# A decoder layer on one core: the last chunk of its sparse FFN selected and summed by tile of 128 rows, and the last batch's window projection issued one head pair per unit

## What is computed

```
h = silu(x @ w_gate) * (x @ w_up)            # 256 x 1024 per batch
g = h.reshape(B, S, I // 4, 4)
_, idx = top_k(abs(g), 2)                    # the two largest of each four
h_sparse = g, with all but those two at zero
out = x + h_sparse @ w_down                  # 1024 -> 256
```

## Time and profile before

| | |
|---|---|
| three runs | 408.34, 408.43 (median), 408.79 us |
| the profiled execution | 408.79 us |
| its span, first to last instruction | 406.9 us |
| mean granted TensorE clock | 0.999 of full |
| busy: PE, PEld, DVE, ACT, POOL | 95%, 78%, 71%, 53%, 42% of the span |
| share of the chain that ended last | PE 54%, DVE 21%, issue 8%, POOL 8%, ACT 7%, DMA 1%, SPq 1% |

### The profile page before, as it was taken

How to read it: one execution, slowest core, us unless ns; L and a number is a source line. 1 busy time by engine, 2 the same in 40 slices (tenths; PEclk the granted TensorE clock), 3 DMA queues, 4 the chain that set the end, 5 groups by cost and what they waited for, 6 DMA issues and landing times.

```text
span 406.9 us, 8265 instructions
## 1 busy us (share of the span) xinstructions
PE 387.9 (95%) x3060; PEld 317.9 (78%) x3060; DVE 288.2 (71%) x616; ACT 214.1 (53%) x546; POOL 169.5 (42%) x168
## 2 busy tenths in 40 slices
PE   8997899799999999999999999999999999998996
PEld 8776778667799877877789877877778779865895
DVE  4986922788859974678959976488867973675373
ACT  1474834397443752287544663186734836187330
POOL 5562698577611430267620440166831420066000
PEclk9999999999999999999999999999999999999999
DMA  7995430213000400343000410243001300200000
GB/s 202 362 346 148 121 117 26 82 50 92 10 15 17 139 2 3 102 118 85 2 15 0 128 31 0 79 119 83 2 2 52 105 0 3 80 0 2 27 0 27
DMA packets 33175, 28.39 MB, mean 70 GB/s; under 512 B 18672, under 2 KB 28016, under 8 KB 32880
## 3 DMA queue, kind: packets, MB, share of 16 engines
q1 hardware_dynamic: 33136, 27.87, 22.3%
HBM read 18.95 MB, written 4.98 MB: 59 GB/s over the span
## 4 chain that ended last, share of the span: by engine, by line
PE 54%; DVE 21%; issue 8%; POOL 8%; ACT 7%; DMA 1%; SPq 1%; POOLq 0%; DVEq 0%; ACTq 0%
PE ps L658 12%; PE ps L739 8%; PE ps L598 5%; DVE rope L966 4%; ACT prob L1394 4%; POOL prob L1255 4%; PE ps L524 3%; DVE mx L996 3%; PE ps L755 3%; PE ps L619 3%; PE ps L533 3%; DVE total L1010 2%; DVE rope L963 2%; PE ps L644 2%; PE ps L697 2%
## 5 line engine op out<-in xcount | busy, mean ns | idle before, releaser
L1255 POOL TENSOR_TENSOR prob<-prob,inv 128x512 f32<-128x512 f32 x80 | 82.7, 1041 | 81.4 <-DVE inv L1016 81.4
L1394 ACT ACTIVATE prob<-ps,mx 128x128 f32<-128x128 f32 (+1 forms) x128 | 52.6, 429 | 16.4 <-DVE mx L994 13.2
L658 PE MATMUL ps<-wo_sb,qs 128*128 128x256 f32 x256 | 59.6, 379 | 0.0
L1248 POOL TENSOR_TENSOR qs<-rope 128x512 f32<-128x512 f32 x32 | 40.8, 1275 | 41.6 <-DVE rope L966 37.7
L598 PE MATMUL ps<-ident_sb,prob 128*128 128x128 f32 x320 | 49.8, 278 | 4.9 <-POOL prob L1255 4.3
L658 PEld LDWEIGHTS ps<-wo_sb,qs 128*128 128x128 f32 x256 | 46.9, 190 | 6.7 <-issue 1.4
L1404 ACT ACTIVATE pT<-ps 128x512 f32<-128x512 f32 x76 | 45.6, 600 | 10.7 <-PE ps L598 10.1
L966 DVE TENSOR_TENSOR rope<-ps,trig_sb 64x512 f32<-64x512 f32 x70 | 48.2, 688 | 0.9
L598 PEld LDWEIGHTS ps<-ident_sb,prob 128*128 128x128 f32 x320 | 36.5, 140 | 13.9 <-POOL prob L1255 9.9
L1231 POOL TENSOR_TENSOR rstd<-vareps,power 128x1 f32<-128x1 f32 x24 | 13.2, 553 | 67.7 <-DVE vareps L945 67.4
L994 DVE TENSOR_REDUCE mx<-ps 128x2 f32<-128x512 f32 (+1 forms) x48 | 32.7, 689 | 9.0 <-PE ps L578 8.1
(11 more groups left out here) (164 smaller groups left out, 798.7 us busy)
## 6 DMA issues: line engine op xcount, KB each, us to landing
k<-kx SPq DMA_DIRECT2D x32, 128.0 KB, 2.9
q<-qx SPq DMA_DIRECT2D x28, 128.0 KB, 2.5
vb<-v_sb SPq DMA_DIRECT2D x42, 64.0 KB, 2.1
work<-in_wgu SPq DMA_DIRECT2D x4, 512.0 KB, 7.8
wo_sb<-in_wo SPq DMA_DIRECT2D x1, 2048.0 KB, 13.4
vb<-v_sb SPq DMA_DIRECT2D x36, 32.0 KB, 2.8
wq_raw<-in_wqk SPq DMA_DIRECT2D x2, 512.0 KB, 7.9
wd_sb<-in_wd SPq DMA_DIRECT2D x1, 1024.0 KB, 7.3
```

The source lines that it names most:

```text
L658: mm = pe.matmul(half_banks(use, b)[:, 0, :], window_o[t][:, pair, r, :], wo_sb[:, pair, r, :], start=(pair == 0 and r == 0), stop=(pair = ...
L1248: pool.tensor_tensor(to, cos, sin, ALU.add).then_inc(s_sums, 1)
L1255: pool.tensor_tensor(p, p, inv[:, i % ND, 0:g].unsqueeze(2).broadcast_to([P, g, 512 // g]), ALU.mult).then_inc(s_norm, 1)
L1394: ins = act.activation(prob[:, i % ND, h * k:(h + 1) * k], ps[:, BANK_S + i % 2, h * k:(h + 1) * k], ACT.Exp, bias=mx[:, i % ND, h:h + 1], ...
```

## The change

It has two parts. In the last batch's window phase, `window_out` of the first tile is called once per round i = 8 to 11, as in the other batches. And the last chunk of the last batch is handled by tile t of 128 rows from the second half of its products on: DVE multiplies lanes 2 and 3 tile by tile, ACT takes their magnitudes tile by tile, DVE compares each tile in four instructions, TensorE adds the ranks of each tile in two banks of its own, DVE keeps each tile, TensorE projects each tile into a bank of its own, DVE adds each and SP writes each. The idle matmuls of the last selection become one, between the two tiles' ranks; the first chunk's projection goes tile by tile too.

```diff
--- before.py
+++ after.py
@@ -75,7 +75,7 @@
 OUT0_AT = 10
 
 IDLE_UNITS = {13: 1, 14: 1}
-IDLE = {"scores": 2, "values": 1, "transposes": 1, "gates": 1, "ranks": 3, "last": 1}
+IDLE = {"scores": 2, "values": 1, "transposes": 1, "gates": 1, "ranks": 1}
 
 HELD_AT = 2
 
@@ -111,6 +111,9 @@
 FFN_BANKS = [(o, i % NF) for i, o in enumerate(FFN_ORDER[:n])]
 FFN_BANKS += [(("gate10", HELD), 0), (("gate11", HELD), 1), (("up11", HELD), 2)]
 FFN_BANKS += [(o, i % NF) for i, o in enumerate(FFN_ORDER[n:])]
+
+LAST_SUMS = ("down", "down_second")
+FFN_BANKS += [((LAST_SUMS[1], B - 1), dict(FFN_BANKS)["gate11", B - 1])]
 FFN_PLACE = {o: (NM + k, sum(l == k for _, l in FFN_BANKS[:i])) for i, (o, k) in enumerate(FFN_BANKS)}
 
 
@@ -313,7 +316,8 @@
             return ps[:, BANKS_M[k] if k < NM else BANK_PT + k - NM, :]
 
 
-        rank_banks = [ps[:, BANKS_M[k], :].rearrange("p (t n) -> p t n", t=2) for k in (0, 2)]
+        rank_banks = [[ps[:, k, 0:2 * P].rearrange("p (t n) -> p t n", t=2) for k in banks]
+                      for banks in ((BANKS_M[0], BANKS_M[2]), (BANK_S, BANK_S + 1))]
 
         def half_banks(name, b):
             return bank(name, b).rearrange("p (t n) -> p t n", t=2)
@@ -474,9 +478,10 @@
                     latents(b + 2)
                 if b + 1 < B:
                     cross_keys(b + 2)
-            wait_drained(sp, "down", B - 1)
-            sp.dma_start(out[B - 1].rearrange("(t p) d -> p t d", p=P), rows[B - 1]).then_inc(s_out, 16)
-            sp.wait_ge(s_out, 16 * B)
+            for t, use in enumerate(LAST_SUMS):
+                wait_drained(sp, use, B - 1)
+                sp.dma_start(out[B - 1][t * P:(t + 1) * P, :], rows[B - 1][:, t]).then_inc(s_out, 16)
+            sp.wait_ge(s_out, 16 * (B + 1))
 
         @block.tensor
         def _(pe):
@@ -758,14 +763,27 @@
                 if 3 in lanes and (c or b < HELD):
                     mm.then_inc(filled(*use), 1)
 
-            def ranks():
+            def down_tile(c, t):
+
+                b, use, tile = B - 1, LAST_SUMS[t], slice(t * P, (t + 1) * P)
+                if c == 0:
+                    claim(use, b)
+                for j in range(4):
+                    pe.wait_ge(s_kept, 4 * (FC * b + c) + (4 * t if c else 0) + j + 1)
+                    mm = pe.matmul(half_banks(use, b)[:, t, :], hidden[b][c][:, j, tile], wd_sb[:, c * 4 + j, :],
+                                   start=(c == 0 and j == 0), stop=(c == 1 and j == 3), skip_group_check=True)
+                if c:
+                    mm.then_inc(filled(use, b), 1)
+
+            def ranks(t):
 
                 pe.wait_ge(s_minus, 1)
-                pe.wait_ge(s_beats, FC * B)
-                b01, b23, b02, b13, b03, b12 = (beats[:, k, :] for k in range(6))
-                first, second = rank_banks
-                pe.matmul(first, ident_bf[:], beats[:, 2:4, :], start=True, stop=False, skip_group_check=True)
-                pe.matmul(first, ident_bf[:], beats[:, 4:6, :], start=False, stop=False, skip_group_check=True)
+                pe.wait_ge(s_beats, FC * B + t)
+                b01, b23, b02, b13, b03, b12 = (beats[:, k, t * P:(t + 1) * P] for k in range(6))
+                first, second = rank_banks[t]
+                pe.matmul(first, ident_bf[:], beats[:, 2:4, t * P:(t + 1) * P], start=True, stop=False, skip_group_check=True)
+                pe.matmul(first, ident_bf[:], beats[:, 4:6, t * P:(t + 1) * P], start=False, stop=False,
+                          skip_group_check=True)
                 pe.matmul(first[:, 0, :], ident_bf[:], b01, start=False, stop=True, skip_group_check=True)
                 pe.matmul(first[:, 1, :], minus_bf[:], b01, start=False, stop=True, skip_group_check=True)\
                   .then_inc(s_ranks, 1)
@@ -791,12 +809,8 @@
                         unit_transpose(b, i - LAG_T)
                     if i == NQB + LAG_V - 1 and more:
                         transpose_norm("ln1", b, 3 * b + 2)
-                    if i >= NQB and more:
+                    if i >= NQB:
                         window_out(b, 0, pair=i - NQB)
-                    elif NQB <= i < NQB + 3:
-                        if i == NQB:
-                            window_out(b, 0, pair=0)
-                        window_out(b, 0, pair=i - NQB + 1)
                     if i >= LAG_V:
                         unit_values(b, i - LAG_V)
                 n = 3 * b + (3 if more else 2)
@@ -892,11 +906,13 @@
                     unit_scores(b + 1, 2)
                     down(b, 0, (2, 3))
                 else:
-                    down(b, 0)
+                    for t in range(TT):
+                        down_tile(0, t)
+                    ranks(0)
                     idle(IDLE["ranks"], BANK_S)
-                    ranks()
-                    idle(IDLE["last"], BANK_S)
-                    down(b, 1)
+                    ranks(1)
+                    for t in range(TT):
+                        down_tile(1, t)
 
             pe.wait_ge(s_warm, 1)
             for _ in range(WARM):
@@ -1023,27 +1039,38 @@
                 dve.tensor_tensor(h, h, half_banks(f"up{c}{j}", b), ALU.mult)\
                    .then_inc(drained(f"up{c}{j}", b), 1)
 
-            def compare(b, c):
+            def last_values(t):
+
+                b, tile = B - 1, slice(t * P, (t + 1) * P)
+                wait_filled(dve, "up11", b)
+                wait_drained(dve, "gate11", b)
+                h = hidden[b][1][:, 2:4, tile]
+                dve.tensor_tensor(h, h, half_banks("up11", b)[:, :, tile], ALU.mult).then_inc(drained("up11", b), 1)
+
+            def compare(b, c, t=None):
 
                 n = FC * b + c + 1
                 mag, to = mags[b][c], held_beats if (b, c) == (HELD, 1) else beats
-                dve.wait_ge(s_mag, 2 * n)
+                if t is not None:
+                    mag, to = (x[:, :, t * P:(t + 1) * P] for x in (mag, to))
+                dve.wait_ge(s_mag, 2 * n + (t or 0))
                 dve.tensor_tensor(to[:, 0:2, :], mag[:, 0::2, :], mag[:, 1::2, :], ALU.is_ge)
                 dve.tensor_tensor(to[:, 2:4, :], mag[:, 0:2, :], mag[:, 2:4, :], ALU.is_ge)
                 dve.tensor_tensor(to[:, 4, :], mag[:, 0, :], mag[:, 3, :], ALU.is_ge)
                 dve.tensor_tensor(to[:, 5, :], mag[:, 1, :], mag[:, 2, :], ALU.is_ge).then_inc(s_beats, 1)
 
-            def keep(src, b, c, lanes=range(4)):
+            def keep(src, b, c, lanes=range(4), rows_of=slice(0, S)):
                 for j in lanes:
                     op, least = ((ALU.is_ge, 2.0), (ALU.is_ge, 1.0), (ALU.is_ge, 0.0), (ALU.is_le, 1.0))[j]
-                    h = hidden[b][c][:, j, :]
+                    h = hidden[b][c][:, j, rows_of]
                     dve.scalar_tensor_tensor(h, src[j], least, h, op, ALU.mult).then_inc(s_kept, 1)
 
-            def keep_last():
+            def keep_last(t):
 
                 for k in range(2):
-                    dve.wait_ge(s_ranks, k + 1)
-                    keep([rank_banks[j // 2][:, j % 2, :] for j in range(4)], B - 1, 1, (2 * k, 2 * k + 1))
+                    dve.wait_ge(s_ranks, 2 * t + k + 1)
+                    keep([rank_banks[t][j // 2][:, j % 2, :] for j in range(4)], B - 1, 1, (2 * k, 2 * k + 1),
+                         slice(t * P, (t + 1) * P))
 
             def pair_sums(b, c, beats, part):
                 n = FC * b + c + 1
@@ -1191,14 +1218,22 @@
                     chunk_values(b, 0, j)
                 if b != HELD:
                     sparsify(b, 0)
-                    for j in range(2):
-                        chunk_values(b, 1, j)
+                    chunk_values(b, 1, 0)
+                    if more:
+                        chunk_values(b, 1, 1)
                 if more:
                     first_units(b + 1, b)
                 else:
-                    compare(b, 1)
-                    keep_last()
-                    add_out("down", b, b)
+                    for t in range(TT):
+                        last_values(t)
+                    for t in range(TT):
+                        compare(b, 1, t)
+                    for t in range(TT):
+                        keep_last(t)
+                    for t, use in enumerate(LAST_SUMS):
+                        wait_filled(dve, use, b)
+                        dve.tensor_tensor(rows[b][:, t], half_banks(use, b)[:, t, :], rows[b][:, t], ALU.add)\
+                           .then_inc(drained(use, b), 1)
 
             dve.memset(warm, 0.0).then_inc(s_warm, 1)
             dve.memset(kd[:, :, :, 0:WIN], 0.0)
@@ -1449,6 +1484,13 @@
                     act.wait_ge(s_beats, FC * b + c)
                 act.activation(mags[b][c][:, 2 * j:2 * j + 2, :], hidden[b][c][:, 2 * j:2 * j + 2, :], ACT.Abs)\
                    .then_inc(s_mag, 1)
+
+            def last_magnitudes(t):
+
+                k, n = ring_use("up11", B - 1)
+                act.wait_ge(s_drained[k], n + 1 + t)
+                tile = slice(t * P, (t + 1) * P)
```

(7 more changed lines are left out.)

## The result

The changed kernel took 406.08 us in the median (405.84 to 407.13, 6 runs), the one before 408.61 beside it (408.34 to 409.93, 6 runs): ratio 0.9935, 95% interval 0.9920 to 0.9951. That is 2.5 us less, where 1.95 was forecast. A second set gave 406.40 against 408.67 (ratio 0.9949, 0.9933 to 0.9965).

What follows compares the result with a forecast made beforehand. TensorE, busy 95% of the span, was taken as the bound, with a serial ladder in the last selection; 0.64 + 0.65 + 0.27 + 0.39 = 1.95 us takes the median 408.43 to 406.5, range 405.7 to 407.5.

Steps and rivals of the forecast that it cites:

- The projection in step: Last batch's window phase: one pair before each unit's values, the 0.81 us stall goes, gates begin 0.64 us earlier.
- The cover of the later norm: Norm behind wo0: ready near 337.5, wanted by TensorE at 339.9 in the new order, so 2.4 us of cover left.
- The rival that this gain is lost on the way: A transfer or the chain of units around 350 to 380 us takes up the projection's gain: 407.1, chance 0.13.
- Comparisons and keeps: Last selection on DVE: a tile's comparisons 1.10 us, two passes 0.23 more than one; keeps some 0.20 apart.
- The ranks: Last selection on TensorE: 128-column matmuls 0.08 apart, a tile's ranks 0.85 us, last chunk's matmuls begin 0.65 earlier.
- The bound of 1.04: Last chunk's earlier start if 128-column rank matmuls take 0.053 each: 1.04 us gained.
- The end: Behind the last matmul: last addition 0.42 instead of 0.69, gaining 0.27 us; last write half the data, gaining 0.39.
- the tail gives little: Rival at the tail: 128-column ranks cost as 256-column ones, 0.65 becomes 0.21: 406.9, chance 0.14.
- It doesn't do what it says: Rival: tiles follow each other without overlap and wo0 is waited for: 408.2, chance 0.06.
- The slower clock: Rival: with fewer fillers TensorE's clock falls before the last chunk, its 16 records take 3.46 more: 409.9, chance 0.05.

Runs made afterwards that it cites:

- the late ranks: Changed kernel with TensorE taking tile 0's ranks only when both tiles are compared: 407.45 us, ratio to the kernel before 0.9970.

## Why the prediction was right, and where a size was off

**The projection in step** was right to a few hundredths. Forecast from unit 5's transposes: unit 7's values at 10.67 us, the gates at 11.30, the addition of wo0 at 10.74; measured 10.67, 11.27 and 10.78. The cover of the later norm was 2.4 us as worked out.

**The rival that this gain is lost on the way** didn't come true; whether a small part is lost stays open. Between the issue of the queries' second write (L409) and the first read back (L416), the trip through DRAM took 2.08 us in one trace and 2.65 in another (2.08 to 2.70 over all). SP's rows with one write at the end, and then with three idle matmuls, edits that lie 50 us later:

```profile
346.87 0.70 SPq L409 DMA_DIRECT2D qx<-k_lo  x1
348.95 2.87 SPq L416 DMA_DIRECT2D q<-qx  x4
```

```profile
346.64 1.26 SPq L409 DMA_DIRECT2D qx<-k_lo  x1
349.29 2.85 SPq L416 DMA_DIRECT2D q<-qx  x4
```

Over the eleven traces with the step, the first chunk's projection comes 68.20 to 68.91 us behind unit 5's transposes, mean 68.50; over the three without, 69.00 to 69.15, mean 69.06. So 0.57 of the 0.68 arrives on average. The scatter goes with the trip: the two longest (2.65 and 2.70) have 68.91 and 68.72, the two shortest (2.08 and 2.10) 68.21 and 68.20. With only three traces without the step, the missing 0.1 can't be told from this scatter, but all eleven with the step lie below all three without, so the gain isn't lost. The 0.82 in the changed kernel's first trace had a short trip (2.16) in it, which is luck.

**Comparisons and keeps** came as worked out: 1.10 forecast for a tile and 1.08 measured, keeps 0.20 apart. Two passes take 2.23 from the first comparison's start to the second beats, one took 1.97, so the cut costs DVE 0.26; the 0.23 of the prediction is a slip, for by its own times it is 2.28 against 1.97. The Trainium skill (VectorE: DVE Perf Modes, "The TRN2 errata") says that small tiles pay the fixed cost once per tile. This case's rows agree: comparisons follow each other after 0.34 us at 256 elements and 0.20 at 128, so some 0.07 of each doesn't shrink. One reading of the prediction was wrong: that this is paid where TensorE has other work. The kernel without the idle matmul shows TensorE waiting 0.4 for tile 1's comparisons, so the 0.26 is on the path. It isn't seen in the sum, for the comparisons also begin earlier, 2.46 behind the first chunk's projection and not 2.75: tile 0 needs only half of the last product and magnitude.

**The ranks** are the term that was mis-sized: 0.65 forecast for the last chunk's earlier start, 1.02 measured. No row had shown bf16 matmuls of 128 columns, and I took the middle of 0.053 and 0.107. They follow each other after 0.055, so a tile takes 0.66, not 0.85, and the idle matmul costs 0.07 of the path, not 0.18. The bound of 1.04 that stood beside the forecast was almost met. The Trainium skill (TensorE: Matmul & The Clock Gate, "Back-to-back issue gap") gives 81 ns for a pair of weight load and matmul of 128 columns. That doesn't hold in this stretch, with 0.055 us.

**The end:** the addition is 0.27 shorter as forecast, but the last chunk takes 3.72 us to the addition's start instead of 3.65, so 0.20 is left; as in the run without the idle matmul behind the ranks, its first weight load begins only 0.05 ahead of the matmul, not 0.21. The write gave 0.47 in this trace and 0.43 on average, where 0.39 was forecast: its data.

The forecast of 1.95 and the measured 2.5 differ by more than the ranks' 0.37. On average over the traces the stages give 0.57 + 1.02 + 0.20 + 0.43 = 2.2; the rest is the scatter of the transfer and of the runs (2.3 in the second set). The upper end of the range, 407.5, is 408.43 less 0.87 and should read 407.6; nothing hangs on it.

Of the other rivals, "the tail gives little" had the ranks at the wrong end. "It doesn't do what it says" is what the late ranks built, and there nothing was left at that stage: the overlap was real. The slower clock didn't come, even without fillers.

## What to carry to other kernels

At the tail of a kernel, where the engines work one after another on one block, cutting the block in two pays what one engine can do on the first half beside another's work on the second (here half of the ranks, 0.65), and the last addition and write are shorter too. The fixed part of each further instruction is to be set against it (here 0.26, on the path). A filler is free only while it covers a wait: the first idle matmul cost 0.07, each further one 0.43. A new order has to be counted with the waits that it opens: keeping tile 0 earlier lost 0.09 until the pause behind tile 1's ranks was covered, and gained 0.16 then. When a term rests on a form that no row shows, work out both bounds and see whether another instruction then hides the difference.

## What the hardware showed that was not expected

TensorE's clock. In six of the fourteen traces, of several of these kernels, the mean granted clock was 0.996 and unit 5's transposes of the last batch began at 325.05 to 325.37 us; in the other eight they began at 323.92 to 324.42. The changed kernel's first trace is one of the six (columns as above):

```profile
30.00:32.00 2.00, 1.20 (x5) 0.77 (x6) 0.32 (x1) 2.00 (x8) 1.27 (x1) 1.00 0.35 72
32.00:34.00 2.00, 2.00 (x10) 1.91 (x10) 0.07 (x1) 0.18 (x2) 0.00 (x0) 0.58 0.56 78
34.00:36.00 2.00, 2.00 (x11) 1.86 (x11) 1.33 (x3) 0.62 (x2) 0.00 (x0) 0.57 0.87 336
```

0.58 is a stretch mostly at 1.2 GHz. Ahead of it, in 30 to 32, TensorE was busy for only 1.20 of 2 us. The repeat of the same kernel, at full clock there:

```profile
30.00:32.00 2.00, 1.44 (x6) 0.67 (x4) 0.86 (x2) 2.00 (x6) 1.26 (x2) 1.00 0.16 35
32.00:34.00 2.00, 1.57 (x13) 1.48 (x13) 0.21 (x1) 0.73 (x5) 0.23 (x1) 1.00 0.21 49
34.00:36.00 2.00, 1.59 (x14) 1.38 (x13) 1.93 (x4) 0.76 (x2) 0.00 (x0) 1.00 0.89 213
```

TensorE was busy 1.44 us in 30 to 32 there. But that doesn't decide it: over 30 to 32 the six traces have 1.13 to 1.30 us, and of the eight at full clock four have 1.44 or 1.45, the other four 1.13 to 1.22. About 1 us hangs on this, as much as the ranks' term; what decides it wasn't tried and stays open.

It also moves the medians. Of the twelve runs with only the new placing of the pairs, six had a clock of 0.996; the other six have a median of 408.01, and the kernel before's eleven at 0.998 and over beside them 408.80. So the 0.42 by the medians of that part is 0.8 at one clock.

Bf16 matmuls of 128 columns with a weight load each ran 0.055 us apart, half of the 0.107 to 0.11 of those of 256 columns, though each weight load's record is 0.10 us long (397.48 above).
